# One slot of h becomes a fifth slot for rows of C, and TensorE sums one step nearer to VectorE

## The reference

```python
def step(h, inp):
    d_t, B_t, x_t, C_t = inp
    dA = jnp.exp(d_t[..., None] * A)
    h = dA * h + (d_t * x_t)[..., None] * B_t[:, None, :]
    y = jnp.einsum('bdn,bn->bd', h, C_t)
    return (h, y)
```

## Time and profile before

| | us |
|---|---|
| median of 3 runs | 2067.27 |
| lowest, highest | 2060.34, 3051.39 |
| the profiled execution | 2064.06 |
| its span, first to last instruction | 2062.1 |

### The profile page before, as it was taken

How to read it: one execution, slowest core, us unless ns; L and a number is a source line. 1 busy time by engine, 2 the same in 40 slices (tenths; PEclk the granted TensorE clock), 3 DMA queues, 4 the chain that set the end, 5 groups by cost and what they waited for, 6 DMA issues and landing times. The chain is left out here.

```text
span 2062.1 us, 16895 instructions
## 1 busy us (share of the span) xinstructions
PE 1841.0 (89%) x4940; PEld 684.4 (33%) x4940; DVE 1799.4 (87%) x1072; ACT 1150.7 (56%) x1182; POOL 1939.2 (94%) x853
## 2 busy tenths in 40 slices
PE   6898889899898899899899899889889979978777
PEld 2333333333333233233333233333324323323322
DVE  3989897859989988987899997997989998799994
ACT  3757565557557456555755745745674754453331
POOL 1999999999999999999999999999999999899995
PEclk8999999999999999999999899999999989999997
DMA  4568559566766857776766676785667676667683
GB/s 146 197 216 186 211 201 218 187 231 190 205 228 216 214 194 240 177 243 228 186 204 218 199 217 210 214 221 207 204 166 244 215 194 197 219 199 217 224 212 89
DMA packets 125847, 421.95 MB, mean 205 GB/s; under 512 B 18284, under 2 KB 22652, under 8 KB 125756
## 3 DMA queue, kind: packets, MB, share of 16 engines
q1 hardware_dynamic: 125648, 420.82, 67.2%
q10 hardware_dynamic: 108, 0.07, 0.0%
HBM read 410.40 MB, written 6.29 MB: 202 GB/s over the span
## 5 line engine op out<-in xcount | busy, mean ns | idle before, releaser
L894 POOL TENSOR_TENSOR ring<-ring,c_ring 128x1024 f32<-128x1024 f32 x576 | 1345.8, 2361 | 50.3 <-DVE ring L844 45.0
L507 PE MATMUL y_ps<-ring,wp 128*128 128x512 f32 x2304 | 1162.9, 622 | 32.5 <-DVE yv_fwd L824 17.8
L844 DVE TENSOR_TENSOR_SCAN ring<-a_ring,b_ps 128x1024 f32<-128x1024 f32 x379 | 866.2, 2285 | 34.8 <-ACT a_ring L647 1.7
L507 PEld LDWEIGHTS y_ps<-ring,wp 128*128 128x128 f32 x2304 | 431.3, 196 | 548.8 <-issue 449.9
L844 DVE TENSOR_TENSOR_SCAN ring<-b_ps,b_ring 128x1024 f32<-128x1024 f32 x197 | 445.7, 2273 | 66.4 <-ACT b_ps L647 26.9
L491 PE MATMUL b_ps<-b_in,sel 96*64 96x512 bf16 (+1 forms) x1050 | 244.3, 410 | 152.6 <-DVE ring L844 151.7
L647 ACT ACTIVATE a_ring<-delta_ab,wp 128x1024 f32<-128x1024 f32 x233 | 263.0, 1141 | 176.6 <-DVE ring L844 175.9
L888 POOL TENSOR_TENSOR b_ring<-u_ab,b_ring 128x1024 f32<-128x1024 f32 x151 | 356.6, 2362 | 3.1 <-DMA b_ring<-bc_rows 3.0
L807 DVE TENSOR_TENSOR b_ps<-u_ab,b_ps 128x1024 f32<-128x1024 f32 x233 | 282.2, 1211 | 54.7 <-PE b_ps L491 49.2
L647 ACT ACTIVATE b_ps<-delta_ab,wp 128x1024 f32<-128x1024 f32 x151 | 168.5, 1117 | 203.1 <-DVE ring L844 202.6
L640 ACT ACT_TABLE_LOAD x186 | 238.6, 1283 | 71.7 <-DVE ring L844 39.5
(11 more groups left out here) (83 smaller groups left out, 800.7 us busy)
## 6 DMA issues: line engine op xcount, KB each, us to landing
c_ring<-bc_rows SPq DMA_DIRECT2D x384, 512.0 KB, 4.6
c_ring<-bc_rows SPq DMA_DIRECT2D x384, 256.0 KB, 4.4
b_ring<-bc_rows SPq DMA_DIRECT2D x151, 512.0 KB, 5.3
b_ring<-bc_rows SPq DMA_DIRECT2D x92, 256.0 KB, 5.5
bc_rows<-bc_out SPq DMA_DIRECT2D x24, 128.0 KB, 3.7
out<-io SPq DMA_DIRECT2D x16, 192.0 KB, 3.9
io<-x SPq DMA_DIRECT2D x6, 384.0 KB, 6.6
b_in<-parts SPq DMA_DIRECT2D x24, 96.0 KB, 2.3
```

What stands on the lines that cost most here:

```text
L507: nc.tensor.matmul(half(y_ps[:, :], j), ident, half(ring[:, g % RING, :], j), start=(n == 0 and kind != ROWS), stop=(n == NS - 1)).then_in ...
L844: nc.vector.tensor_tensor_scan(out=h, data0=a, data1=b, initial=0.0, op0=ALU.mult, op1=ALU.add).then_inc(h_ready, 1)
L894: nc.gpsimd.tensor_tensor(r, r, c_ring[:, g % C_RING, :], ALU.mult).then_inc(g_ready, 1)
```

## The change

Three numbers change, and with them a fourth place that uses one. The ring of h has five slots in place of six. The ring of C rows has five slots in place of four, and SyncE fetches a row four steps ahead of its own step in place of three. TensorE sums the step three behind its own in place of four, and VectorE takes a finished tile one step earlier, since `take_at` uses SUM_LAG. The memory that both rings take together is the same. At the start, and at the restart after the jobs that stand alone, SyncE fetches four rows of C ahead of the loop in place of three.

```diff
-RING = 6
-C_RING = 4
-C_LEAD = 3
+RING = 5
+C_RING = 5
+C_LEAD = 4
 A_RING = 2
 B_RING = 3
 B_LEAD = 6
@@
 LEAD = {"ahead": 1, "ahead_c": C_LEAD, "ahead_a": 2, "ahead_a2": 1, "ahead_b": 3}
 SP_LEAD = dict(LEAD, ahead_b=B_LEAD)
-SUM_LAG = 4
+SUM_LAG = 3
 SKIP_AT = 10
```

## The result

The changed kernel takes 2073.86 us (median of 8 runs, 2071.85 to 2076.23); the kernel before takes 2064.97 us over 8 runs. One of these eight, 3051.39 us, lies far outside all others and is not in the ratio, which goes by the other seven (median 2064.32). The ratio is 1.0046, with a 95% interval of 1.0035 to 1.0056: 0.5% slower, a small difference, but clear of the noise. The forecast was 2074 us.

What follows compares the result with a forecast made beforehand. The prediction took POOL as the bound. Late sums costing 12.6 us less 2.4 us won on C gave +10.2 us on 2064.06 us, so 2074 us, range 2066 to 2084 (chance 0.53).

Steps and rivals of the forecast that it cites:

- What bounds: POOL, busy 1939.2 of 2062.1 us, is the bound; a change can only win time in which POOL stands still.
- The slot of h: Ring of h, six slots to five: the slot comes free at the same place of TensorE's program as before.
- The C part: C rows fetched one step earlier by SyncE: POOL's waits for C shrink, winning 2.4 us (0 to 4.8).
- The late sums: TensorE's sum waits for product s-3 in place of s-4; delays through full stretches reach POOL, costing 12.6 us (0 to 58).
- seven places: Late sums whose following stretches lack TensorE idle time: losses of 3.8, 2.3, 1.3, 1.9, 1.2 (two sums) and 2.1 us.
- the prediction's rule: At TensorE's late sums: where TensorE idles soon after, nothing is lost; example 2.9 us late, 1.10 us idle.
- the lag is hidden: Rival: every late sum is absorbed and only the C waits change; 2059 us at best, range 2058 to 2066, chance 0.25.
- VectorE is throttled everywhere: Rival: each of POOL's 48 scan waits grows by one line 807 operation; 2122 us, 2.8% slower, chance 0.06.
- The clock rival: Rival: TensorE's clock falls to 1.2 GHz after the new waits, costing 12 us more; 2086 us, chance 0.14.
- Waits for C under 1 us: Sign in the profile after: POOL's waits for rows of C fall from 4.8 us to under 1.
- TensorE's waits grown by over 10 us: Sign: line 507's waits for POOL's line 894 grow by 10 us or more, with single waits of 2 to 4 us.
- Waits for the scan at 55 to 60 us: Sign in the profile after: POOL's waits for VectorE's scan rise from 45.0 to 55 or 60 us.

Runs made afterwards that it cites:

- the slot alone: Five slots of h in place of six, lag of four and four C slots kept, against the kernel before: 2180.38 us, ratio 1.0564.
- the lag alone: SUM_LAG 3 in place of 4, with six slots of h and four of C, against the kernel before: 2077.42 us, ratio 1.0069.
- the run that only makes room: Kernel before without the z gate weights and one x * D matrix, freeing memory and computing other numbers: 2058.7 us, ratio 0.9977.
- seven stretches kept: Kernel before with a lag of three, but four kept in seven stretches (95 of 576 steps): 2068.41 us, ratio 1.0017.

## Why the prediction was right

**What bounds.** Held. POOL's busy time did not move (1939.2 and 1939.8 us), and the whole change in time is POOL's standing still. The one row of C more at the start cost nothing, as forecast: the first product starts within 0.01 us of where it did.

**The slot of h.** Held. Six slots or five make no difference beside a lag of three (1.0069 and 1.0066). That the two moves belong together is shown from the other side by the slot alone, 1.0564.

**The C part.** The mechanism held, and the size in part by luck. SyncE's program kept its place and each row went out one issue earlier. In the changed kernel, SP and POOL where POOL waited 1.66 us before:

```profile
965.96 0.32 SPq L443 DMA_DIRECT2D c_ring<-bc_rows  x1
...
967.27 4.99 SPq L394 DMA_DIRECT2D dt_in<-parts  x6
...
973.65 0.59 SPq L443 DMA_DIRECT2D c_ring<-bc_rows  x1
...
977.45 9.30 POOL L894 TENSOR_TENSOR ring<-ring,c_ring 128x1024 f32<-128x1024 f32 x4
```

The gathers of dt still take 5 us, but the row that used to go out right behind them now goes out ahead of them, at 965.96, and the one that was late takes its place behind them, at 973.65, and POOL passes with four products in a row. The term was put at 2.4 us, half of 4.8, because the other half would be lost to the scan; the half was chosen and not counted. By the start of the same products 0.8 and 1.7 us stayed, 2.5 us. The other two gains, 1.5 and 1.1 us, were taken back at the next product. Around the first, POOL after the change

```profile
163.51 4.66 POOL L894 TENSOR_TENSOR ring<-ring,c_ring 128x1024 f32<-128x1024 f32 x2 [1.01 <-DVE ring L844]
...
169.62 2.36 POOL L894 TENSOR_TENSOR ring<-ring,c_ring 128x1024 f32<-128x1024 f32 x1 [1.45 <-DVE ring L844]
```

and before it

```profile
161.72 2.36 POOL L894 TENSOR_TENSOR ring<-ring,c_ring 128x1024 f32<-128x1024 f32 x1 [0.98 <-DVE ring L844]
...
165.51 4.67 POOL L894 TENSOR_TENSOR ring<-ring,c_ring 128x1024 f32<-128x1024 f32 x2 [1.43 <-DMA c_ring<-bc_rows]
```

The wait of 1.43 us for C is gone, and 1.45 us for the scan stands one product later, beside the 0.98 us for the scan that stood there already.

**The late sums.** The mechanism held: 12.6 us counted at seven places, 12.7 measured there, each place within 0.8 us. Keeping the lag of four at these places alone gave 9 of 13 us back. That the two sums meet within 0.1 us is luck, since a single place can be off by one or two microseconds without the change. Two parts were not right. The single waits of TensorE were put at 2 to 4 us; the longest is 2.1 (2.7 at the weight loads, from which the prediction measured), since the lateness is met in pieces at several sums. And late sums at steps 30 to 36 of items 4 and 7, by the prediction's own measure up to 2.9 us late, were counted as nothing. They cost 2.9 us in the changed kernel and 4.6 with the lag alone. VectorE and POOL in item 4 with the lag alone:

```profile
853.29 1.23 DVE L807 TENSOR_TENSOR b_ps<-u_m,b_ps 128x1024 f32<-128x1024 f32 x1 [1.83 <-PE b_ps L491]
...
873.16 2.36 POOL L894 TENSOR_TENSOR ring<-ring,c_ring 128x1024 f32<-128x1024 f32 x1 [1.00 <-DVE ring L844]
```

VectorE waits 1.83 us for the broadcast of step 37. From step 32 to step 37 its scans fall from 2.2 to 4.7 us behind those of the kernel before, and since VectorE has no idle time after that, they stay so until POOL's stock of h has run out at step 42. The sums at steps 38 to 41, up to 3.0 us late, add nothing to VectorE's 4.7 us: there the prediction's rule held that TensorE's idle time absorbs them. What was missing is the same question for VectorE: what it has lost before TensorE idles, it must make up by idle time of its own.

**What evened it out.** 12.7+2.9-2.5 = 13.1 us, and the products end 9.0 us later. The missing 4 us are the balance of gains and losses at single steps elsewhere. The largest is a gain of 2.3 us at step 11 of item 1. POOL there, before and after:

```profile
253.19 2.37 POOL L894 TENSOR_TENSOR ring<-ring,c_ring 128x1024 f32<-128x1024 f32 x1 [2.67 <-DVE ring L844]
...
254.62 2.36 POOL L894 TENSOR_TENSOR ring<-ring,c_ring 128x1024 f32<-128x1024 f32 x1 [0.41 <-DVE ring L844]
```

There TensorE and VectorE set the time, VectorE was only 1.4 us later than before (249.51 and 250.93 for the same operation), and POOL, 3.7 us behind until then, gave back the rest. With the lag alone POOL is 2.1 us behind ahead of this step and level with the kernel before after it: what it lost in item 0 is gone. The prediction's sum let every loss last to the end. Two more gains, 1.6 us at step 4 and 1.3 at step 11 of item 2, appear in the run that only makes room too, so they are not the change's. So the closeness of 2074 to 2073.86 owes something to chance: the sum left out 2.9 us of loss and about 4 us that came back.

**The rivals.** That the lag is hidden falls with the run of the lag alone. That VectorE is throttled everywhere falls for a lag of three, but it describes a lag of two, where POOL's waits for the scan number 102 in place of 48. The clock rival falls: in the steps of all seven places in the table the granted clock is 1.00, before and after. The stretches behind the first two, after the change (busy us by engine, clock, DMA share, GB/s), beside the earlier trace rows:

```profile
85.00:130.00 45.00, 43.49 (x120) 17.72 (x119) 36.94 (x21) 24.74 (x25) 45.00 (x21) 1.00 0.63 211
...
304.00:356.00 52.00, 49.25 (x145) 18.04 (x146) 36.45 (x21) 26.58 (x27) 48.47 (x22) 1.00 0.77 192
```

Elsewhere some of the new waits were followed by the lower clock, but the time at that level as a whole fell (see the last section). So the rival's cost is not there; the prediction's reason against it, which went by the length of the waits, does not hold. A further rival, not in the prediction, is the read of the finished tile, which moved with the lag. VectorE's waits for it rose from 10.1 to 13.0 us with the lag alone. But 8.7 us of these are two reads in item 2, where POOL falls no further behind, and in the faster kernel with seven stretches kept they are 18.3 us. So they do not carry the loss. Last, the prediction took 2% for about what a measurement can tell from no change; the interval of the ratio here, 1.0035 to 1.0056, is 0.2% wide.

**The profile's signs.** Waits for C under 1 us: they are gone. TensorE's waits grown by over 10 us: from 2.8 to 33.5. Waits for the scan at 55 to 60 us: 62.4, a little over.

## What to carry to other kernels

Where one engine's queue waits for another's product, lay the two traces side by side step by step and ask of each late wait whether the waiting engine, and then the next one, has idle time before the bounding engine runs dry; the waits without it are the ones to count before anything is built. Here this gave 12.6 us beforehand, and missed 2.9 us where VectorE had none. A delay counted so can still come back later, where the bounding engine has to wait in any case. A ring's length and the lag of its consumer are one number in two places: taking a slot away cost 116 us by itself and nothing once the consumer moved with it. A wait taken off the bounding engine is worth its length only if the next thing that engine waits for is not already due.

## What the runs showed of the hardware that was not expected

The mean granted clock of TensorE did not fall with the new waits; it rose, from 0.958 to 0.966 in the profiled executions. Over the runs on record it lies between 0.953 and 0.963 for the kernel before and between 0.962 and 0.966 for the changed kernel. Over the profiled span the time at the 1.2 GHz level fell from 175 to 140 us. The Trainium skill, "TensorE: Matmul & The Clock Gate", Part 1, has idleness bring the lower clock back; here more waiting in shorter pieces went with less of it. Whether the shorter pieces are the reason was not tried. The length of a wait alone does not tell what follows it. TensorE's waits of 1.84 and 0.91 us near 306 us were followed by a clock of 1.00, and in the kernel before 2.75 us of idleness before 161.70 by 1.00 and 2.67 us before 829.40 by 0.50. Two of the new waits for POOL in the changed kernel, and the clock in the stretch behind each (0.57 and 1.00):

```profile
551.64 1.64 PE L507 MATMUL y_ps<-ring,wp 128*128 128x512 f32 x2 [2.08 <-POOL ring L894]
...
551.64:555.04 3.40, 3.40 (x6) 1.09 (x8) 3.31 (x3) 1.15 (x1) 3.40 (x2) 0.57 0.59 169
...
1362.56 1.13 PE L507 MATMUL y_ps<-ring,wp 128*128 128x512 f32 x2 [2.08 <-POOL ring L894]
...
1362.56:1365.96 3.40, 3.40 (x10) 1.30 (x11) 3.31 (x3) 1.15 (x1) 3.40 (x2) 1.00 0.58 137
```
